# The gate by Tanh instead of Sigmoid, row norms and batch preparation moved to other quads, roots in two pieces

## The reference

```python
def attn(x, weight):                       # 16 heads of 8 channels
    y = x.reshape(b, t, 16, 8).transpose(0, 2, 1, 3)
    scores = jnp.einsum('bhtk,bhsk->bhts', y, y) / math.sqrt(8)
    attn = jax.nn.softmax(scores, axis=-1)
    o = jnp.einsum('bhts,bsc->bhtc', attn, x)      # every head weighs all 128 channels
    return o.transpose(0, 2, 1, 3).reshape(b, t, 16 * c) @ weight

def ffn(x, W_r, W_k, W_v, mu_r, mu_k):
    x_prev = x shifted by one token
    xr = mu_r * x + (1.0 - mu_r) * x_prev
    xk = mu_k * x + (1.0 - mu_k) * x_prev
    r = jax.nn.sigmoid(xr @ W_r.T)
    return r * (jnp.square(jax.nn.relu(xk @ W_k.T)) @ W_v.T)

x = x + _layernorm(attn(_layernorm(x)))
x = x + _layernorm(ffn(_layernorm(x)))
```

## Time and profile before

| | us |
|---|---|
| runs | 992.82, 991.94, 987.48; median 991.94 |
| the profiled execution, its own time | 988.09 |
| its span | 986.3 |
| first Exp starts | 13.5 |
| last Exp starts | 941.7 |
| TensorE busy | 915.8 (93%) |
| VectorE busy | 858.7 (87%) |
| ScalarE busy | 761.6 (77%) |
| GpSimd busy | 308.7 (31%) |

### The profile page before, as it was taken

The page is one execution under the profiler, slowest core; times in us unless marked ns, Lnnn a source line. Parts: engine busy times, 40 slices in busy tenths (PEclk is TensorE's granted clock), DMA queues, the critical chain, the costliest instruction groups (busy, mean ns, idle before and its releaser), DMA issues.

```text
span 986.3 us, 17700 instructions
## 1 busy us (share of the span) xinstructions
PE 915.8 (93%) x5979; PEld 438.9 (44%) x5979; DVE 858.7 (87%) x1125; ACT 761.6 (77%) x1045; POOL 308.7 (31%) x490
## 2 busy tenths in 40 slices
PE   3789999999999999999999999999999999999992
PEld 2234444544444444444444444444444444444451
DVE  6579998889889998889898899979989898988976
ACT  5378778877888788878877879787788878777764
POOL 2012221442124521534117531265114441173210
PEclk9789999999999999999999999999999999999996
DMA  5699999989888988899897898988989897988830
GB/s 137 143 223 196 202 192 206 208 190 201 172 176 177 188 163 171 166 230 203 170 184 161 183 182 164 182 197 194 205 164 188 184 189 160 186 164 180 168 65 22
DMA packets 99466, 173.50 MB, mean 176 GB/s; under 512 B 21297, under 2 KB 62129, under 8 KB 99377
## 3 DMA queue, kind: packets, MB, share of 16 engines
q0 software_dynamic: 36720, 133.71, 70.3%
q1 hardware_dynamic: 62656, 38.67, 14.3%
HBM read 28.12 MB, written 10.49 MB: 39 GB/s over the span
## 4 chain that ended last, share of the span: by engine, by line
PE 58%; POOL 11%; ACT 9%; issue 9%; DVE 8%; DMA 5%; SPq 1%; DVEq 0%; POOLq 0%; ACTq 0%
PE ps_o L587 16%; PE ps_o L588 14%; PE ps_o L589 14%; POOL fnw L387 7%; PE ps_s L568 6%; ACT e_f L746 5%; DMA e_hi<-e_f 4%; DVE e_lo L1076 3%; PE ps_r L604 2%; PE ps_r L602 2%; PE ps_r L603 2%; POOL e_hi L422 2%; POOL nw L387 1%; ACT part L758 1%; ACT L746 1%
## 5 line engine op out<-in xcount | busy, mean ns | idle before, releaser
L1076 DVE TENSOR_TENSOR e_lo<-e_f,e_hi 128x2048 f16<-128x2048 f32 x256 | 584.9, 2285 | 60.9 <-DMA e_hi<-e_f 60.2
L746 ACT ACTIVATE e_f<-ps_s 128x2048 f32<-128x2048 f32 x256 | 481.7, 1882 | 143.3 <-PE ps_s L568 136.1
L587 PE MATMUL ps_o<-e_hi,y_hi 128*128 128x512 f16 x1024 | 394.3, 385 | 6.1 <-DVE o_neg L1082 6.0
L588 PE MATMUL ps_o<-e_lo,y_hi 128*128 128x512 f16 x1024 | 391.9, 383 | 0.0
L589 PE MATMUL ps_o<-e_hi,y_lo 128*128 128x512 f16 x1024 | 391.3, 382 | 0.0
L422 POOL DMA_DIRECT2D e_hi<-e_f x255 | 139.2, 546 | 615.4 <-ACT e_f L746 557.9
L758 ACT ACTIVATE part<-ps_r,rden 128x128 f32<-128x128 f32 x508 | 144.4, 374 | 33.3 <-DVE rden L1088 32.9
L587 PEld LDWEIGHTS ps_o<-e_hi,y_hi 128*128 128x128 f16 x1024 | 100.1, 98 | 157.3 <-issue 59.1
L589 PEld LDWEIGHTS ps_o<-e_hi,y_lo 128*128 128x128 f16 x1024 | 100.7, 98 | 123.3 <-issue 3.9
L588 PEld LDWEIGHTS ps_o<-e_lo,y_hi 128*128 128x128 f16 x1024 | 100.8, 98 | 93.3 <-issue 3.5
L568 PE MATMUL ps_s<-op_t,op_s 32*128 32x512 f16 x1024 | 103.0, 389 | 30.5 <-ACT e_f L746 25.4
(11 more groups left out here) (216 smaller groups left out, 456.5 us busy)
## 6 DMA issues: line engine op xcount, KB each, us to landing
e_hi<-e_f POOLq DMA_DIRECT2D x255, 512.0 KB, 4.9
op_t<-scr_t SPq DMA_DIRECT2D x504, 32.0 KB, 3.7
op_s<-scr_s SPq DMA_DIRECT2D x504, 16.0 KB, 3.2
scr_s<-yT SPq DMA_DIRECT2D x12, 256.0 KB, 4.5
scr_t<-yT SPq DMA_DIRECT2D x12, 256.0 KB, 5.6
out_dram<-res SPq DMA_DIRECT2D x7, 256.0 KB, 4.5
xs<-in_L_attn_x_dram SPq DMA_DIRECT2D x3, 512.0 KB, 6.9
scr_s<-eighth SPq DMA_DIRECT2D x4, 256.0 KB, 4.2
```

What stands on the lines that cost most here:

```text
L587: nc.tensor.matmul(dst, y_hi[:, b % 2, s, :], e_hi[:, ring, g, :], start=(q == 0 and g == 0), stop=False)
L588: nc.tensor.matmul(dst, y_hi[:, b % 2, s, :], e_lo[:, ring, g, :], start=False, stop=False)
L746: nc.scalar.activation(e_f[:, k % EF_RING], ps_s[:], ACT.Exp, scale=1.0 / ROOT).then_inc(weighed, 1)
L1076: dve.tensor_tensor(flat(e_lo[:, ring]), flat(e_f[:, k % EF_RING]), flat(e_hi[:, ring]), ALU.subtract).then_inc(split, 1)
```

## The change

- The gate is Tanh of half its argument instead of Sigmoid. Where the product with the gate is made, VectorE computes (gate + 1) * value in one scalar_tensor_tensor instruction instead of gate * value, and `w_v` is taken in with the factor 0.5, by a second ScalarE instruction in quad 12.
- The two ScalarE norms of a row, four blocks each at offsets 7 and 36, become two blocks each at offsets 8 and 10, and 36 and 38.
- GpSimd's roots of a row, three pieces at three offsets from 4, 12 and 33, become two pieces at offsets from 4, 14 and 34: first 2 instructions, then 5 or 7.
- In the rest of the row: VectorE's add, sums and moments of the second norm 9, 10, 11 -> 11, 12, 13; gate 23 -> 24, key 24 -> 25, Relu 25 -> 26, Square 26 -> 28, value 28 -> 29, product 30 -> 31, its sums and moments 31, 32 -> 32, 33, the last add 38 -> 39, the store 40 -> 41. For the last spread row the rows end at the same offset 36 as before.
- Batch preparation, by the offset k%64: sums 14 to 17 -> 12, 13, 17, 18; moments 18 -> 22; root 19 to 21 -> 25 to 27; normalize 22, 23 -> 30, 31; split 24 -> 34; low part by GpSimd 28 -> 35; Square by ScalarE 26 -> 38; squares by VectorE 32 -> 44; `turn_y` of the high part 43 -> 41 and of the low part 45 -> 49; `take_y` 44, 46 -> 42, 52; `turn_top` 47 -> 45, `spread_top` 49 -> 47, `batch_top` 48 -> 46, `batch_bound` 50 -> 48, `batch_shift` 52 -> 49; `turn_shift` 54 -> 53, `take_shift` 55 -> 54; marks 47 -> 52; SyncE's `keep_hi` 45 -> 43, `keep_lo` 47 -> 53, `keep_shift` 56 -> 55. New waits among them keep `ps_x` from being overwritten.

The core of the diff:

```diff
-SPAN = 41
+SPAN = 42
+FFN_NORM = 36
...
             def row_part(o, r):
-                for i, first in enumerate((4, 12, 33)):
-                    if 0 <= o - first < 3:
-                        root_row(i, r, o - first)
+                for i, first in enumerate((4, 14, 34)):
+                    if o == first:
+                        root_row(i, r, 0)
+                    if o == first + 1:
+                        root_row(i, r, 1)
+                        root_row(i, r, 2)
...
             def row_part(o, r):
-                if o in (7, 36):
-                    i, src, dst, done_ = (0, acc[:, r % 2], xn, a_normed) if o == 7 else (2, gated, res, f_normed)
+                if o in (8, 10, FFN_NORM, FFN_NORM + 2):
+                    i, src, dst, done_ = (0, acc[:, r % 2], xn, a_normed) if o < FFN_NORM else (2, gated, res, f_normed)
+                    u = int(o in (10, FFN_NORM + 2))
                     act.wait_ge(f_root[i], root_steps(i) * (r + 1))
...
-                    for k in range(RB):
+                    for k in range(PAIR * u, PAIR * (u + 1)):
                         ins = nc.scalar.activation(dst[:, k, :], src[:, k, :], ACT.Identity, scale=fnw[:, i, 1, k:k + 1],
                                                    bias=fnw[:, i, 3, k:k + 1])
...
-                if o == 23:
+                if o == 24:
                     act.wait_ge(gate_ps, r + 1)
                     ge(act, f_gated, r)
-                    nc.scalar.activation(flat(gate[:]), ps_x[:], ACT.Sigmoid).then_inc(gate_ok, 1)
+                    nc.scalar.activation(flat(gate[:]), ps_x[:], ACT.Tanh, scale=0.5).then_inc(gate_ok, 1)
-                if o == 25:
+                if o == 26:
...
-                if o == 26:
+                if o == 28:
...
-                nc.scalar.activation(wT[:].rearrange("p i c -> p (i c)"), ps_x[:, 0:3 * P], ACT.Copy).then_inc(f_ready, 1)
+                nc.scalar.activation(wT[:, 0:2, :].rearrange("p i c -> p (i c)"), ps_x[:, 0:2 * P], ACT.Copy).then_inc(f_ready, 1)
+                nc.scalar.activation(wT[:, 2, :], ps_x[:, 2 * P:3 * P], ACT.Copy, scale=0.5).then_inc(f_ready, 1)
...
-                if o == 30:
+                if o == 31:
                     dve.wait_ge(kv_ps, r + 1)
                     dve.wait_ge(gate_ok, r + 1)
-                    dve.tensor_tensor(flat(gated[:]), flat(gate[:]), ps_x[:], ALU.mult).then_inc(f_gated, 1)
+                    dve.scalar_tensor_tensor(out=flat(gated[:]), in0=flat(gate[:]), scalar=1.0, in1=ps_x[:], op0=ALU.add,
+                                             op1=ALU.mult).then_inc(f_gated, 1)
...
-                    if o in (22, 23):
-                        batch_normalize(b, range(4 * (o - 22), 4 * (o - 22) + 4))
-                    if o == 24:
+                    if o in (30, 31):
+                        batch_normalize(b, range(4 * (o - 30), 4 * (o - 30) + 4))
+                    if o == PER_ROW + 2:
                         batch_split(b)
-                    if o == PER_ROW:
+                    if o == PER_ROW + 12:
                         batch_squares(b)
+                    if o == PER_ROW + 14:
+                        batch_top(b)
                     if o == PER_ROW + 16:
-                        batch_top(b)
-                    if o == PER_ROW + 18:
                         batch_bound(b)
-                    if o == PER_ROW + 20:
+                    if o == PER_ROW + 17:
                         batch_shift(b)
```

More of the change, by code:

```diff
@@ L215, in rows_at @@
                     now = [QUADS - first + 2 * (k - QUADS) + i for i in range(2)]
-                found += [(r, o) for o in now if 0 <= o < (SPAN if r < LAST_ROW - 1 else SPAN - 5)]
+                found += [(r, o) for o in now if 0 <= o < (SPAN if r < LAST_ROW - 1 else FFN_NORM)]
             return found
@@ L459, in _ @@
                 if b is not None:
[L460 to L462 removed]
+                    if 25 <= o < 28:
+                        root_batch(b, o - 25)
+                    if o == PER_ROW + 3:
                         low_batch(b)
[L464 removed]
+                    if o == PER_ROW + 20:
                         mark_batch(b)
@@ L507, in turn_shift @@
                 pe.wait_ge(shift_ok, b + 1)
+                if b:
+                    pe.wait_ge(yT_ready, 2 * b + 2)
                 for k in range(NB):
@@ L664, in _ @@
                 if b is not None:
-                    if o == PER_ROW + 11:
+                    if o == PER_ROW + 9:
                         turn_y(b, 0)
                     if o == PER_ROW + 13:
+                        turn_top(b)
+                    if o == PER_ROW + 15:
+                        spread_top(b)
+                    if o == PER_ROW + 17:
                         turn_y(b, 1)
[L669 to L673, removed]
+                    if o == PER_ROW + 21:
                         turn_shift(b)
@@ L914, in last_sigmoid @@
                 act.wait_ge(f_gated, LAST_ROW)
-                nc.scalar.activation(flat(gate[:, pair(u), :]), half_ps("gate", u), ACT.Sigmoid).then_inc(l_gate, 1)
+                nc.scalar.activation(flat(gate[:, pair(u), :]), half_ps("gate", u), ACT.Tanh,
+                                     scale=0.5).then_inc(l_gate, 1)
             def last_relu(u):
@@ L929, in _ @@
             last_sqrt(0, slice(0, RB), HALVES)
-            row_part(36, LAST_ROW - 1)
+            for o in (FFN_NORM, FFN_NORM + 2):
+                row_part(o, LAST_ROW - 1)
             last_sqrt(1, slice(0, RB), 1)
-            nc.scalar.activation(idle[:], consts[:, 0:1], ACT.Sigmoid)
+            nc.scalar.activation(idle[:], consts[:, 0:1], ACT.Tanh)
             for u in range(HALVES):
@@ L1014, in batch_bound @@
                                        top_ps(b)[:, 0:H].unsqueeze(1).to_broadcast([P, NB, H]), ALU.mult))
-                near_root(y, v)
+                step(dve.tensor_scalar(y.bitcast(I32), v.bitcast(I32), 1, None, ALU.logical_shift_right))
+                dve.tensor_scalar(y.bitcast(I32), y.bitcast(I32), float(ROOT_BITS), None, ALU.add).then_inc(bounded, 1)
             def batch_shift(b):
+                dve.wait_ge(bounded, b + 1)
                 dve.tensor_scalar(shx[:].rearrange("p k (h c) -> p (k h) c", c=HS),
@@ L1207, in _ @@
                 if b is not None:
-                    if 14 <= o < 18:
-                        batch_sums(b, range(2 * (o - 14), 2 * (o - 14) + 2))
-                    if o == 18:
+                    if o in (12, 13, 17, 18):
+                        first = 2 * (12, 13, 17, 18).index(o)
+                        batch_sums(b, range(first, first + 2))
+                    if o == 22:
                         batch_moments(b)
-                    if o in (22, 23):
-                        batch_normalize(b, range(4 * (o - 22), 4 * (o - 22) + 4))
-                    if o == 24:
+                    if o in (30, 31):
+                        batch_normalize(b, range(4 * (o - 30), 4 * (o - 30) + 4))
+                    if o == PER_ROW + 2:
                         batch_split(b)
-                    if o == PER_ROW:
+                    if o == PER_ROW + 12:
                         batch_squares(b)
+                    if o == PER_ROW + 14:
+                        batch_top(b)
                     if o == PER_ROW + 16:
-                        batch_top(b)
-                    if o == PER_ROW + 18:
                         batch_bound(b)
-                    if o == PER_ROW + 20:
+                    if o == PER_ROW + 17:
                         batch_shift(b)
@@ L1308, in last_gated @@
                 dve.wait_ge(l_gate, u + 1)
-                dve.wait_ge(f_normed, LAST_ROW)
-                dve.tensor_tensor(flat(gated[:, pair(u), :]), flat(gate[:, pair(u), :]), half_ps("kv", u),
-                                  ALU.mult).then_inc(l_gated, 1)
+                dve.wait_ge(f_normed, HALVES * LAST_ROW)
+                dve.scalar_tensor_tensor(out=flat(gated[:, pair(u), :]), in0=flat(gate[:, pair(u), :]), scalar=1.0,
+                                         in1=half_ps("kv", u), op0=ALU.add, op1=ALU.mult).then_inc(l_gated, 1)
                 dve.wait_ge(l_gated, u + 1)
```

42 lines of the change are left out of this document (22 added, 20 removed).

## The result

The whole change takes 987.30 us (median of 20 runs, 977.12 to 993.18), the kernel before 990.85 (20 runs, 986.28 to 994.92): a ratio of 0.9949, 95% interval 0.9926 to 0.9973. Two of the changed kernel's 20 runs (992.50 and 993.18) count as slow ones and are left out of the ratio, which is why the ratio lies under that of the medians (0.9964). So it is faster, by 0.5%, where 1.6% was forecast, and its median is outside the range by 0.3 us. Its profiled execution took 987.6 us, with a span of 985.8, beside 988.09 and 986.3.

A forecast was written before the change was run, and what follows sets the result against it. TensorE was taken to set the pace, so only its waits could go: -4.9 -9.5 -1.1 +4.2 -0.6 -2.0 = -13.9, 974.2 against the profiled 988.09; half of the median's 3.9 excess added gave 976.0 us, range 966 to 987.

The forecast's parts named there:

- What bounds the kernel: TensorE sets the pace; the change can only remove its waits, 25.1 us between 137 and 941.7 us.
- Gate, -4.9: At the gate, Tanh needs no table load beside Exp, so TensorE's six waits of 0.81 us go.
- the rival of own loads: At the gate, Tanh needs its own loads, 13 loads stay and 4 of the 4.9 us stay: 980, chance 0.10.
- Norm of xn, -9.5: Two blocks (0.83 us) in each of two even quads fit ScalarE's 1.32 idle; TensorE's waits there go, 9.5 us.
- Norm of res, -1.1: Last norm of a row: the root's wait grows to 1.5 to 3.8 us; TensorE waits 1.8 in place of 2.9.
- Longer pieces, +4.2: Casts queued behind longer GpSimd root pieces come later; TensorE waits 0.7 us more in each of six rows.
- the cover of 1.6: Behind the late cast, its products had 1.6 us of cover, of which 1.4 was the xn wait that goes.
- Batch part, -0.6 and -2.0: Batch preparation moved: two small ScalarE waits go (-0.6); VectorE's waits fall from 7.2 to 5.2 us (-2.0).
- root pieces hold up the casts: Rival: both pieces of a row end one `e_lo` later than taken, +27.6 us, 1001.8 by the profiled execution; chance 0.08.

The follow-up runs named there:

- e4: The whole change with the Newton step after pow left out of GpSimd's roots (part of the computation missing): 956.87 us, 0.9662 of the kernel before.
- e6: The whole change with the five Newton-step instructions of GpSimd's roots replaced by five memsets: 957.13 us, 0.9718 of the kernel before.
- e1: The kernel before with the Tanh gate alone, nothing moved: 984.45 us, 0.9941 of the kernel before.
- e2: The whole change with the root of a row's first norm (xn) in three pieces again: 976.38 us, 0.9872 of the kernel before.
- e11: The kernel before with its roots in two pieces at the same first offsets, nothing else: 996.14 us, 1.0101 of the kernel before.
- e8: The kernel before with batch preparation alone moved as in the change: 977.62 us, 0.9913 of the kernel before.
- f1: The whole change unaltered, timed beside its parts on a fourth chip: 980.85 us, 0.9913 of the kernel before.
- f4: The whole change with three-piece roots for both ScalarE norms and the last norm two quads later: 968.13 us, 0.9796 of the kernel before.

## Why the prediction was wrong

**What bounds the kernel:** right in the main. TensorE's waits were most of what there was to gain, and the runs with the fewest waits (e4, e6) take 957 us, 31 less than the profiled execution before. That is 6 us more than the 25.1 that I called the most that the loop can give. Between the spans of before (986.3) and e4 (955.1), 24.5 us are waits behind quad 32, 2.1 lie before the Exp of quad 32, 1.7 are the stretch of low clock, and some 3 more in the loop are placed by no view. I had no term for the clock: the two blocks of the earlier trace rows have it full, and the one low stretch lies at 891.5.

**Gate, -4.9:** right. 5.8 us in e1, within its interval. Tanh needs no load beside Exp, and the rival of own loads is out: there is no load in the loop.

**Norm of xn, -9.5:** right. ScalarE no longer waits for that root, and TensorE waits at no place behind it.

**Norm of res, -1.1:** this is the step that failed, in two terms. The root's wait was bounded at 1.5 to 3.8; it measured 2.0 to 4.2. I then let 1.3 us of lateness be absorbed, taken from the row before, where the wait of 0.73 and `take_y` stood. In the changed kernel 2.02 + 0.88 - 1.32 is 1.6 late, and TensorE waits 0.83: only some 0.75 are absorbed. And I took 0.3 "near the lower end" of 0 to 2.0, because one row had its free window there; the six rows wait 0.83 to 3.05, 1.7 on the mean. Measured: 10.4 us in place of my 1.8, +7.5 against before in place of -1.1.

**Longer pieces, +4.2:** the mechanism and the cover were right, the size was not. The waits at k%32 = 18 are 9.0 us, and e2, which removes them, is 4 to 8 us faster by the ratios than the whole change. The cast of quad 14 comes 1.1 to 3.8 us later than in the same row before (I had 1.1 to 3.4), and in a seventh row, the first, 5.1 later. Where it is under 1.8 later, TensorE does not wait, as the cover of 1.6 said; where it is 1.8 to 5.1 later, it waits 0.7 to 3.2. I took 0.7 a row from 0 to 3.2; it measured 1.3 over seven rows, because in three of them the cast comes 3.5 to 5.1 us later. That the late cast of quad 12 adds to it is not shown: in e2 it is late and costs nothing at 18, in e11 it is on time and TensorE waits there all the same. e11 shows the price of such pieces by themselves, at the old offsets: 10 us. I also had no term for batch work on TensorE that waits for VectorE behind the late cast (3.5 us after, 6.4 in e11).

**Batch part, -0.6 and -2.0:** right in sign, off by a factor of three. I moved 7.2 to 5.2; e8 has 0.2. Work in the odd quads instead of the even ones takes it out of the way of `o_neg`, as I had written, but I gave the clump behind the token mix a price that no row had shown. In the whole change 4.4 us of such waits are there again; that the late casts bring them back is likely, as e8 has none, but was not tried.

**The total:** the forecast left TensorE 11.2 us of waits (1.8 at the `res` norm, 4.2 behind the casts, 5.2 of VectorE's own); there are 23.8 (10.4, 9.0 and 4.4). Of the 12.6 too many, 8.6 are the step on the `res` norm, 4.8 the step on the longer pieces; the rest came out 0.8 better. The two further stretches of low clock, 3.4 us, are a term that the sum did not have. So the profiled execution came 13.4 us over the forecast 974.2: 12.6 of waits, 3.4 of clock, and 2.6 less elsewhere. The rival "root pieces hold up the casts", with its point at 1.6 us later than before, came: five of seven rows are past that point, three of them far past it. With a cover of 1 us each it was worked out to 990; the profiled execution took 987.6. I gave it 0.08. But the nearness is in part luck: the larger share of the loss, 8.6 us, went through ScalarE's wait for the root and not through the casts.

## What to carry to other kernels

Where one engine issues what everything else waits for (here GpSimd with the casts), do not put more small work in front of an issue than one gap holds without costing it; a piece should be costed by how many long neighbours it can fall behind, not by its own length, and at the upper bound when it may fall behind one more. Look at the granted clock as well as at the waits: here a wait of some 2 us could bring 1.7 us more of low clock behind it. And time the parts of a change one by one: roots in two pieces alone cost 10 us, the gate and the batch part alone gained 6 and 9, and together with the rest they made 0.5 to 0.9%.

## What the runs showed of the hardware that was not expected

GpSimd's tensor_tensor of 128x4 (add or multiply) takes 0.20 us when nothing is in its way and 2.0 on the median when it begins under an `e_lo`; memsets in its place take 105 ns and let the kernel run as if nothing stood there: 0.972 of before in place of 0.991 to 0.995, about 2%, for five instructions a root that read or do not read. The kernel's ratio for the same edit was 0.9949, 0.9909 and 0.9913 in three timings on different chips, as far apart as effects of 4 us: differences of that size between e and f runs of different chips are not settled by these runs, and f1 to f4 were set side by side for that reason.
